# A four-layer graph network on one Trainium2 core: the relational layer sums its rows per basis and projects afterwards

## The reference, cut to what matters

```
layer 1 (gcn): out = A (relu(A (x W1)) W2), A x = segment_sum(edge_weight * x[src], dst), W1 128x256, W2 256x128
layer 2 (rel): W_r = sum_b comp[r, b] V_b           8 relations, 4 bases, V_b 128x128
               proj = einsum(ni,rio->nro, x, W)
               out = relu(x root + segment_sum(proj[src, edge_type], dst) + bias)
layer 3 (hyp): h = logmap0(x) W + b; out = relu(expmap0(relu(segment_sum(edge_weight * h[src], dst))))
layer 4 (att): xp = x W as 8 heads of 16; a graph attention with leaky relu,
               a softmax over the edges of each destination, out = sum(alpha * xp[src]) + bias
```

## Time and profile before

| | |
|---|---|
| median of 3 runs | 12424.98 us (12419.63 to 12438.84) |
| the profiled execution | 12429.37 us, span 12427.5 us |
| mean granted clock of TensorE | 0.777 |
| busy over the span | TensorE 7799.2 us (63%), VectorE 6243.7 (50%), POOL 5933.2 (48%), ScalarE 2586.6 (21%) |
| gathers of layer 2 | 1568, 946 ns each |
| gathers of layer 4 | 1592, 1031 ns each |

### The profile page before, as it was taken

How to read it: one execution, slowest core, us unless ns; L and a number is a source line. 1 busy time by engine, 2 the same in 40 slices (tenths; PEclk the granted TensorE clock), 3 DMA queues, 4 the chain that set the end, 5 groups by cost and what they waited for, 6 DMA issues and landing times. The chain is left out here.

```text
span 12427.5 us, 276718 instructions
## 1 busy us (share of the span) xinstructions
PE 7799.2 (63%) x88297; PEld 6807.8 (55%) x88297; DVE 6243.7 (50%) x21526; ACT 2586.6 (21%) x7283; POOL 5933.2 (48%) x5927
## 2 busy tenths in 40 slices
PE   5858999979999974222222337777734555555555
PEld 5857888868888852222222336666633444444443
DVE  8975666646666652111111345555563444444446
ACT  3542222222222231000000111111112322232323
POOL 2324444424444414666666425555523555555552
PEclk8879999999999986556555669999976655655555
DMA  1024454434554453111111224334321111111113
GB/s 34 0 59 115 120 120 117 120 108 119 120 120 118 121 162 118 45 45 46 45 45 46 70 83 106 103 103 105 103 76 47 39 39 39 39 39 39 39 39 61
DMA packets 906850, 968.13 MB, mean 78 GB/s; under 512 B 141573, under 2 KB 801261, under 8 KB 906413
## 3 DMA queue, kind: packets, MB, share of 16 engines
q1 hardware_dynamic: 721094, 574.77, 16.4%
q0 software_dynamic: 185216, 386.21, 13.3%
q10 hardware_dynamic: 487, 6.55, 0.2%
HBM read 838.94 MB, written 134.46 MB: 78 GB/s over the span
## 5 line engine op out<-in xcount | busy, mean ns | idle before, releaser
L469 POOL DMA_INDIRECT ring<-att_table,idx x1592 | 1641.0, 1031 | 1212.4 <-ACT idx L460 755.0
L469 POOL DMA_INDIRECT ring<-rel_table,idx x1568 | 1484.0, 946 | 782.7 <-issue 463.2
L1160 PE MATMUL psum<-state,ring 128*128 128x128 bf16 x24420 | 1636.4, 221 | 184.2 <-issue 150.4
L534 PE MATMUL psum<-sel,ring 128*128 128x128 f32 x3136 | 648.7, 395 | 1637.4 <-DVE sel L503 993.4
L1160 PEld LDWEIGHTS psum<-state,ring 128*128 128x128 bf16 x24420 | 1406.8, 99 | 385.1 <-issue 279.4
L1114 DVE TENSOR_SCALAR state<-iota_row,state 128x128 f32<-128x128 f32 x5684 | 1543.4, 357 | 4.8 <-PE psum L1174 4.8
L534 PEld LDWEIGHTS psum<-sel,ring 128*128 128x128 f32 x3136 | 613.8, 302 | 1672.8 <-DVE sel L503 1015.6
L1306 POOL DMA_INDIRECT state<-hyp_table,state x980 | 937.9, 957 | 796.2 <-ACT state L1383 556.1
L1093 POOL DMA_INDIRECT ring<-gcn_table,idx x812 | 787.3, 970 | 893.2 <-ACT idx L1138 754.1
L1093 POOL DMA_INDIRECT ring<-rows,idx x812 | 786.2, 968 | 895.1 <-ACT idx L1138 755.9
L1107 DVE TENSOR_SCALAR ring<-state,iota_col 128x640 bf16<-128x640 bf16 x1628 | 566.9, 390 | 1210.6 <-DMA state<-drow 839.9
(11 more groups left out here) (404 smaller groups left out, 13342.8 us busy)
## 6 DMA issues: line engine op xcount, KB each, us to landing
state<-xparts SPq DMA_DIRECT2D x1207, 192.0 KB
state<-drow SPq DMA_DIRECT2D x814, 160.0 KB
rel_table<-tout SPq DMA_DIRECT2D x98, 512.0 KB, 2.6
state<-srow SPq DMA_DIRECT2D x393, 96.0 KB
ring<-rows SPq DMA_DIRECT2D x70, 448.0 KB
ring<-att_table,idx POOLq DMA_INDIRECT x1592
ring<-rel_table,idx POOLq DMA_INDIRECT x1568
xparts<-state SPq DMA_DIRECT2D x35, 672.0 KB, 3.6
```

Of the source, the lines that this page charges most:

```text
L469: pool.indirect_dma_start(out=ring[:, u, k, 0:width], out_offset=None, in_=table, in_offset=bass.IndirectOffsetOnAxis(ap=idx[:, u, k:k + 1 ...
L534: last = nc.tensor.matmul(psum[:, u % 2, 0:WIN], ring[:, u, k, 0:D], sel[:, u % 2, k, :], start=(k == 0), stop=(k == K - 1))
L1160: last = nc.tensor.matmul(rowsP[v][:, j * P:(j + 1) * P], reach[v][:, t, j * P:(j + 1) * P], xwin[v][:, t, i, :], start=(t + i == 0), stop ...
```

## The change

**Layer 2.** The stage `project("rel")`, the table, `Wrel` and `gather_pass` are taken out. POOL gathers the rows of the layer's input, `rows1`, by source alone, with DEEP = 7 slots in flight instead of 4 (three of them in `state`). Per group VectorE makes `is_type` (128 x 64), the selection in one step (128 x 1024, comparing with the numbers 0 to 127 kept in PSUM), `shares` (128 x 256: type by basis by relation), their reduction to `share` (128 x 32, in PSUM), and `based` (128 x 4096: the selection times the share of each basis). TensorE sums eight matmuls of 512 columns (`basis_sums`), ScalarE copies the 128 x 512 sums to SBUF and then stages the index of group n + 7, TensorE multiplies by the four V_b into another bank (`projected`, issued behind the next group's `basis_sums`), and VectorE adds the window.

**`residual_norm`**: SP loads three blocks ahead; for layer 2 TensorE turns the loaded rows itself, a block ahead, and ScalarE copies that from PSUM instead of from `state`.

**`gcn_dense`**: the hidden values have two buffers, and the first product is issued a block ahead of the second.

**`project("hyp")`**: staging and turning two blocks ahead, `rows_out` (the old L1896 step) one block ahead.

**Layer 4**: a second exponential writes the edges' weights to PSUM (bank 3), where `messages` reads them; `select` compares with numbers held in the same bank instead of in SBUF.

```diff
+DEEP = 7
+TURN = 2 * DEEP
+assert NG % RING == 0 and NG % TURN == 0
...
-                    out=ring[:, u, k, 0:width], out_offset=None, in_=table,
+                    out=rows[u][:, k, 0:width], out_offset=None, in_=table,
...
+        with pool.Fori(0, NG // deep) as it:
+            for u in range(deep):
+                gather(it * deep + u, u)
...
+based = [state[:, v * K * BASES * WIN:(v + 1) * K * BASES * WIN].rearrange(
+    "p (k b j) -> p k b j", b=BASES, j=WIN) for v in range(2)]
+far = state[:, 2 * K * BASES * WIN:2 * K * BASES * WIN + (DEEP - RING) * K * D].rearrange(
+    "p (u k f) -> p u k f", k=K, f=D)
+deep_rows = [ring[:, u, :, :] if u < RING else far[:, u - RING, :, :] for u in range(DEEP)]
...
+    tout_f = tout[:, :, :].rearrange("p a w -> p (a w)")
+    is_type = tout_f[:, 0:K * RELS].rearrange("p (k r) -> p k r", r=RELS)
+    shares = tout_f[:, K * RELS:K * RELS * (1 + BASES)].rearrange("p (k b r) -> p k b r", b=BASES, r=RELS)
+    sums = [tout_f[:, (v + 1) * BASES * WIN:(v + 2) * BASES * WIN] for v in range(2)]
+    share = psum[:, 4, 0:K * BASES].rearrange("p (k b) -> p k b", b=BASES)
+    numbers = psum[:, 5, 0:WIN]
+    comps = comp[:, :].rearrange("p (r b) -> p b r", b=BASES)
...
-                    stage_index(it * RING + u, u, act)
+            for u in range(DEEP):
+                stage_index(u, u, act)
+            with act.Fori(0, NG // TURN) as it:
+                for u in range(TURN):
+                    n = it * TURN + u
+                    act.wait_ge(sem("slot"), n + (DEEP + 1))
+                    act.wait_ge(sem("proj"), n + 1)
+                    nc.scalar.activation(sums[u % 2], psum[:, u % 2, :], ACT.Copy
+                                         ).then_inc(sem("tA"), 1)
+                    stage_index(n + DEEP, u % DEEP, act)
...
+                types = typeT[:, bass.ds(n * K, K)].unsqueeze(2).to_broadcast([P, K, RELS])
+                a = c.mark(nc.vector.tensor_tensor(
+                    is_type, types, iota_row[:, 0:RELS].unsqueeze(1).to_broadcast([P, K, RELS]),
+                    ALU.is_equal))
+                b = c.mark(nc.vector.tensor_tensor(
+                    sel[:, v, :, :], numbers.unsqueeze(1).to_broadcast([P, K, WIN]),
+                    dstrel[:, bass.ds(n * K, K)].unsqueeze(2).to_broadcast([P, K, WIN]), ALU.is_equal))
+                c.need(a)
+                c(nc.vector.tensor_tensor(
+                    shares, is_type.unsqueeze(2).to_broadcast([P, K, BASES, RELS]),
+                    comps.unsqueeze(1).to_broadcast([P, K, BASES, RELS]), ALU.mult))
+                c(nc.vector.tensor_reduce(share, shares, axis=AX.X, op=ALU.add))
+                c.need(b)
+                dve.wait_ge(sem("slot"), n + (DEEP - 1))
+                nc.vector.tensor_tensor(
+                    based[v], sel[:, v, :, :].unsqueeze(2).to_broadcast([P, K, BASES, WIN]),
+                    share.unsqueeze(3).to_broadcast([P, K, BASES, WIN]), ALU.mult
+                ).then_inc(sem("selected"), 1)
...
+            select(1, 1)
...
+                    select(n + 2, u % 2)
                     b = dve.value_load(base_i[0:1, bass.ds(n, 1)], min_val=0, max_val=N)
-                    dve.wait_ge(sem("slot"), n + RING + 1)
+                    dve.wait_ge(sem("proj"), n + 3)
                     dve.wait_ge(sem("added"), n + 2)
                     win = acc[:, bass.ds(b, WIN)]
-                    nc.vector.tensor_tensor(win, win, psum[:, u % 2, 0:WIN], ALU.add
+                    nc.vector.tensor_tensor(win, win, psum[:, 2 + u % 2, 0:WIN], ALU.add
                                             ).then_inc(sem("added"), 1)
+                c.end()
...
+            def basis_sums(n, u, landed):
+                pe.wait_ge(sem(f"g{u % DEEP}"), landed)
+                pe.wait_ge(sem("selected"), n + 1)
+                pe.wait_ge(sem("tA"), n + 1)
+                for k in range(K):
+                    last = nc.tensor.matmul(
+                        psum[:, u % 2, :], deep_rows[u % DEEP][:, k, 0:D],
+                        based[u % 2][:, k, :, :].rearrange("p b j -> p (b j)"),
+                        start=(k == 0), stop=(k == K - 1))
+                last.then_inc(sem("slot"), 1)
+            def projected(n, v):
+                pe.wait_ge(sem("tA"), n + 3)
+                pe.wait_ge(sem("added"), n + 1)
+                for b in range(BASES):
+                    last = nc.tensor.matmul(psum[:, 2 + v, 0:WIN], Vs[:, b, :],
+                                            sums[v][:, b * WIN:(b + 1) * WIN],
+                                            start=(b == 0), stop=(b == BASES - 1))
+                last.then_inc(sem("proj"), 1)
...
+                    basis_sums(n, u, it * (32 * K) + ((at + u) // DEEP * (16 * K) + 16 * K))
+                    if at + u or not isinstance(it, int):
+                        projected(n - 1, (u - 1) % 2)
...
+    hid = [stage, tout_flat[:, 0:2 * BW].rearrange("p (h w) -> p h w", w=BW)]
...
+            def first_product(b):
...
+            def one(it, u, more):
+                b = it * 2 + u
+                if more:
+                    first_product(b + 1)
...
+            first_product(0)
+            peeled(pe, one)
...
+            for b in range(3):
+                load(b, b % 2)
+            with sp.Fori(0, NB // 2 - 2) as it:
                 for u in range(2):
-                    load(it * 2 + (u + 2), u)
+                    load(it * 2 + (u + 3), 1 - u)
...
-                    nc.scalar.activation(xT[:, u, :], state[:, cols], ACT.Copy)
+                    act.wait_ge(sem("xTready"), b + 1)
+                    nc.scalar.activation(xT[:, u, :], pblk(2 + u), ACT.Copy)
...
+                def rows_turned(it, u):
+                    pe.wait_ge(sem(f"xin{u}"), it * 16 + 16)
+                    pe.wait_ge(sem("staged"), it * 2 + (u + 1))
+                    for t in range(BT):
+                        last = nc.tensor.transpose(pblk(2 + u)[:, t * P:(t + 1) * P],
+                                                   xblk[:, u, t * P:(t + 1) * P], ident[:, :])
+                    last.then_inc(sem("xTready"), 1)
+                def one(it, u, more):
+                    b = it * 2 + u
+                    if kind == "rel" and more:
+                        rows_turned(it + u, 1 - u)
+                    pe.wait_ge(sem("staged"), b + (3 if kind == "rel" else 1))
...
                 cols = bass.ds(b * BW, BW)
-                if more:
+                if kind == "hyp" and not isinstance(it, int):
+                    stage_block(b + 2, u)
+                if kind != "hyp" and more:
...
+                    if more:
+                        rows_out(it + u, 1 - u)
+                    if not isinstance(it, int):
+                        xT_block(b + 2, u)
...
+    exps = psum[:, E_BANK, 0:K * HEADS].rearrange("p (k h) -> p k h", h=HEADS)
+    numbers = psum[:, E_BANK, P:P + WIN]
...
-                nc.scalar.activation(ring[:, u, :, D:ROW5], heads(elog), ACT.Exp
-                                     ).then_inc(sem("ex"), 1)
+                nc.scalar.activation(ring[:, u, :, D:ROW5], heads(elog), ACT.Exp)
+                nc.scalar.activation(exps, heads(elog), ACT.Exp).then_inc(sem("ex"), 1)
...
                 nc.vector.tensor_tensor(
-                    sel_of[u], iota_row[:, :].unsqueeze(1).to_broadcast([P, K, WIN]),
+                    sel_of[u], numbers.unsqueeze(1).to_broadcast([P, K, WIN]),
...
-                    ring[:, u, :, D:ROW5].unsqueeze(3).to_broadcast([P, K, HEADS, CH]),
+                    exps.unsqueeze(3).to_broadcast([P, K, HEADS, CH]),
...
-    project("rel")
-    segment_sum(rel_table, relT, None)
+    bases_sum(rows1)
```

253 lines of the change are left out of this document (90 added, 163 removed).

## The result

The changed kernel takes 12440.4 us in the median of 20 runs, the kernel before 12434.1 us in the median of 20: a ratio of 1.0015, 95% interval 1.0008 to 1.0022. No change was the least likely of the three outcomes forecast. The profiled execution took 12471.9 us, span 12470.1, 31 us above the median of its kernel; stage by stage it is compared with the span of before, so the table shows some 36 us more than the medians do.

A forecast was written before the change was run, and what follows sets the result against it. POOL's gathers were taken to pace the second layer's edge sum, with one stall per ring turn. Terms -194 - 12 - 245 - 57 - 21 - 53 = -582 took 12429.4 to 11847, less 4 to the median 11843 us; range 11650 to 12130.

The forecast's parts named there:

- Projection gone, -194: Layer two's projection that fills the relation table: removed, and nothing hides this stage, so -194 us.
- prelude, -12: Combined matrices no longer built in one VectorE chain, and a cheaper copy: -12 us.
- gcn_dense, -21: Dense steps: double-buffered hidden values take a block from 8.22 to 6.6 us, -21 us; bounds 0 and -23.
- Projection of layer 3, -53: Hyperbolic projection: working two blocks ahead takes a block from 10.36 to 6.5 us, -53 us; bounds -20 and -68.
- Edge sum, -245: Second layer's edge sum: POOL stays the pace at 10.2 us a group, stage 2020 us, -245 us; bounds -310 and 0.
- rival B: Edge sum: late TensorE signals in the new round trip, 13.8 us a group, +706 us, 12549 us; chance 0.05.
- C: Rival of a low granted clock in the edge sum, slower than the kernel before; chance 0.04.
- Residual step, 0: Second layer's residual step: VectorE paces it at about 6 us a block and covers the added transposes, 0 us.
- Attention, -57: Attention layer: the middle between POOL's time coming back, -164, and a second exponential on the path, +50: -57 us.
- rival D: Attention takes the other end: +50 gives 11950 us (chance 0.12), -164 gives 11736 us.
- All else 0: Stages without a term of their own, the first and third layers' edge sums among them: no change, 0 us.
- The chance of no change, 0.01: Whole kernel: a still worse edge-sum pace ends within 25 us of 12425 us; chance 0.01.

The follow-up runs named there:

- e10b: Changed kernel with edge-sum gathers of 32 values a row instead of 128, on the chip with signals on time: edge sum 1994 us, 10.05 us a group.
- e2: Changed kernel with the edge sum's gathers replaced by SyncE's plain loads from fixed places: 8.08 us a group.
- e9: Changed kernel with residual turning behind the product, add one selection later, attention's old steps, 76 padding instructions, on the chip with signals on time: ratio 0.978 to kernel before.
- e12: The changed kernel unedited, run again on a chip with late signals: ratio 1.0021 to the kernel before.
- e14: The kernel of e9 once more, on a chip with late signals: ratio 0.9872 to the kernel before.
- e1: Changed kernel with four slots instead of seven in the edge sum, loop turns of four groups instead of fourteen: stage 2418 us, 12.24 us a group.
- e6: Changed kernel with VectorE's add in the edge sum one selection later: stage 2374.8 us, 11.79 us a group.
- e4: Changed kernel with residual-step turning behind the product and the attention's selection reading numbers from SBUF: residual step 162.3 us, against 217.5 in e1.

## Why the prediction was wrong

- *Projection gone, -194; prelude, -12; gcn_dense, -21:* -194.5, -14.2, -24.2. Right, by their own steps (8.22 less 6.6 is 1.6 us a block and 23 in all, not 21). gcn_dense's blocks after, for the earlier trace rows: 6.5 and 6.1 us apart.

```profile
2650.86 3.29 PE L1558 MATMUL psum<-weights,tout 128*128 128x128 f32 x28
...
2657.38 3.29 PE L1558 MATMUL psum<-weights,ring 128*128 128x128 f32 x28
...
2663.51 3.29 PE L1558 MATMUL psum<-weights,tout 128*128 128x128 f32 x28
```

- *Projection of layer 3, -53:* -31.2. The mechanism held, the term was mis-sized: a block takes 8.1 and 7.5 us, not 6.5. VectorE waits 2.9 us for TensorE's product alone, where I had counted one hand-over for the whole block. For the earlier trace rows, after:

```profile
7202.43 1.90 DVE L1934 SCALAR_TENSOR_TENSOR tout<-psum,rown,bhyp 128x128 f32<-128x128 f32 x7 [2.92 <-PE psum L1893]
...
7210.56 1.90 DVE L1934 SCALAR_TENSOR_TENSOR tout<-psum,rown,bhyp 128x128 f32<-128x128 f32 x7 [2.91 <-PE psum L1893]
...
7218.09 1.90 DVE L1934 SCALAR_TENSOR_TENSOR tout<-psum,rown,bhyp 128x128 f32<-128x128 f32 x7 [2.31 <-PE psum L1893]
```

- *Edge sum, -245:* +144.7. The step that failed is the one on the new waits: "8.6 us, until that selection is ready. It is needed 13 us after that point at a 10 us pace: covered". It put TensorE's signals at no delay, and they were late: 15.5 us in the mean, beyond the 13, and so 12.3 us a group instead of 10.2. Where signals are on time the stretch takes 8.5 and 8.6 us (e10b, e2) and the stage 1994 and 1999 us (e10b, e9), so the rest of the step is right to 1.3%. The lateness was in rival B, at 0.05. What kept its chance low was "where TensorE is kept busy with gathers beside it, ScalarE's copies waited [...] 0.57 us each": that row is of a layer in which POOL has gaps (two times 787 us in 3358, busy 47%). The row that fitted, signals 17.9 us late in a stage where POOL streams, was before me, and I set it aside because slots would cover it. Slots cover POOL's wait; they don't cover VectorE's wait for the small products with the next selection behind it. B's price, 13.8 us a group, was above the 12.3 measured. C, the 0.04 in the chances, stood for a low granted clock: no run shows one near 0.5 over this stage, it was 0.84, and 0.99 in e2.
- *Residual step, 0:* +73.7. "VectorE paces it at about 6 us a block and covers them" counted the transposes' time and not their wait: the turning of block b + 1 waits for a load, and block b's product is queued behind it on TensorE. I had asked that question of the add and not here.
- *Attention, -57:* +61.2, beyond rival D's +50. Gathers came back to 946 ns as said. The step that failed is "I take the middle": the two chains don't meet halfway. POOL wasn't the path, and shorter gathers didn't help. D blamed the second exponential; the runs give the selection from PSUM 41 to 45 us and the exponential 19 to 74, both together 48 to 49, so the split, and what makes the new steps cost time, stay open. Of the 164 us, the 137 of the gathers' durations came back, the 27 between them hardly: their "issue" idle was 457.4 us before and is 450.6 after. In the trace before, the 551 gathers beside a selection or a `messages` step took 1192 ns in the mean and the others 945; after, with one input of each step in PSUM, 944 and 946. With signals on time the stage is 222 us shorter (e10b against e9), with late ones 49 us longer (e12 against e14).
- *All else 0:* the third layer's sum cost 47 us, with 137 fetches instead of 3 by the place of VectorE's code, which no row of before could show; the first layer's sums moved by 14 us the other way, unexplained.

The chance of no change, 0.01, and the upper end of 12130 priced each risk by itself. That the total came out at nothing is a coincidence of these sizes. Late signals, one queue order and one code place came together with +145, +74, +61 and +47, against 264 us that were saved as forecast.

## What to carry to other kernels

Before a stage is rebuilt around an engine's work, read how late its signals come in that stage, and add that lag to the sum of the new loop, from the engine's signal through the other engines back to it. Here 8.6 us with 13 allowed became 15.5. Three spare slots gave 0.2 us a group (e1: 12.24 without them, 12.04 with), and one hand-over fewer gave 2% (e6). A transfer's wait belongs behind the work that doesn't need it in its queue (55 us of 217 in e4). When a stage that the diff doesn't touch gets slower, look for instruction fetches and for an idle time at the turn of a loop (here 137 fetches and 3.5 us).

## What the runs showed of the hardware

- ScalarE's copy started 4 to 7 us (mean) behind the end of TensorE's product, 13 at the 95th percentile in the changed kernel, while GpSimd issued gathers on the four chips with late signals, with a quarter of the bytes (4.30) as with all (4.64); with half of the gathers it was 0.22 us, with none 0.07.
- VectorE's and ScalarE's recorded signals came 0.01 us behind their instructions in the same stage. A third of them has no record there, but the 80 groups of TensorE's large products that waited for VectorE's `based` started 0.10 us behind it, in the median and at the 95th percentile.
- In one of the five groups of runs, on a chip of its own, TensorE's signals were on time in every stage, and the kernel before took 10737 instead of some 12450 us.
- A shift of VectorE's code took an unedited loop from 137 fetches of instructions to 18 (80 instructions) or 3 (76 and one selection more), and 46 to 74 us out of a stage of some 1800, on the chip with signals on time 133 out of 1363.
